# Choosing experts one sequence at a time, and token rows made by transposing back

## The reference, cut to what matters

```python
x = x + ga * attn(layernorm(x) * (1 + ca) + sa)
h = layernorm(x) * (1 + cb) + sb          # the "token rows", 1024 x 256
scores = sigmoid(h @ w_router)            # 1024 tokens x 32 experts
sfc = scores + corr_bias
# 8 groups of 4 experts; a group's score is the sum of its two best; 4 groups are kept,
# and of their experts the 6 best are chosen
topk_idx = top_k(masked(sfc), 6); topk_w = scores[topk_idx]
x = x + gb * (sum over chosen experts of topk_w * expert(h) + shared_experts(h))
```

## Time and profile before

| what | us |
|---|---|
| median of three executions | 492.85 |
| the profiled execution | 493.19 |
| its span, first to last instruction | 491.2 |
| TensorE busy | 415.0 (84%) |
| VectorE busy | 308.1 (63%) |
| ScalarE busy | 193.7 (39%) |
| GpSimd busy | 134.1 (27%) |

### The profile page before, as it was taken

The page is one execution under the profiler, slowest core; times in us unless marked ns, Lnnn a source line. Parts: engine busy times, 40 slices in busy tenths (PEclk is TensorE's granted clock), DMA queues, the critical chain, the costliest instruction groups (busy, mean ns, idle before and its releaser), DMA issues. The chain is left out here.

```text
span 491.2 us, 5968 instructions
## 1 busy us (share of the span) xinstructions
PE 415.0 (84%) x1835; PEld 296.1 (60%) x1836; DVE 308.1 (63%) x718; ACT 193.7 (39%) x336; POOL 134.1 (27%) x145
## 2 busy tenths in 40 slices
PE   2886765788599999999997786489897999799995
PEld 0342054635377777777775535366586777688885
DVE  3489996779344444444443479878678866765432
ACT  2168573424222222222222145281796079322430
POOL 0162000000467777777777302000000000000000
PEclk9999795789699999999999899599999799799998
DMA  8309967693223323333337287602300000000001
GB/s 286 131 20 353 329 158 182 220 372 164 57 77 103 107 96 105 98 107 99 104 118 246 81 304 269 219 1 64 130 0 2 0 0 1 0 1 19 25 0 44
DMA packets 22877, 57.65 MB, mean 117 GB/s; under 512 B 3266, under 2 KB 14020, under 8 KB 21864
## 3 DMA queue, kind: packets, MB, share of 16 engines
q1 hardware_dynamic: 17432, 42.57, 25.6%
q0 software_dynamic: 5424, 14.82, 9.6%
HBM read 46.87 MB, written 10.51 MB: 117 GB/s over the span
## 5 line engine op out<-in xcount | busy, mean ns | idle before, releaser
L659 PE MATMUL bank<-arena,tile_mem 128*128 x224 | 77.4, 469 | 0.0
L1213 POOL DMA_INDIRECT tile_mem<-h_dram,gidx x57 | 55.6, 975 | 55.7 <-DVE gidx L1576 38.2
L1220 POOL DMA_INDIRECT y_dram<-norm,didx x56 | 55.5, 991 | 25.7 <-issue 14.0
L1592 DVE TENSOR_TENSOR tile_mem<-tile_mem,bank 128x176 f32<-128x176 f32 x56 | 18.9, 338 | 69.4 <-ACT tile_mem L1015 69.4
L1171 POOL TENSOR_TENSOR rstd<-ve,mhalf 128x4 f32<-128x4 f32 x8 | 8.1, 1016 | 197.1 <-DVE ve L1333 197.1
L675 PE MATMUL bank<-arena,tile_mem 88*128 x224 | 57.7, 379 | 0.8 <-DVE tile_mem L1587 0.8
L675 PEld LDWEIGHTS bank<-arena,tile_mem 88*128 88x128 f32 x224 | 42.4, 190 | 15.8 <-issue 1.2
L755 PE MATMUL bank<-x_r,f_r 128*128 128x512 f32 x192 | 48.0, 411 | 4.3 <-DVE arena L1767 3.3
L659 PEld LDWEIGHTS bank<-arena,tile_mem 128*128 128x128 f32 x224 | 39.1, 195 | 12.6 <-issue 1.2
L755 PEld LDWEIGHTS bank<-x_r,f_r 128*128 128x128 f32 x192 | 37.4, 197 | 13.8 <-DVE arena L1767 3.7
L1010 ACT ACTIVATE tile_mem<-bank 128x256 f32<-128x256 f32 x57 | 21.9, 385 | 51.9 <-PE bank L652 51.8
(11 more groups left out here) (248 smaller groups left out, 704.1 us busy)
## 6 DMA issues: line engine op xcount, KB each, us to landing
arena<-w_gu SPq DMA_DIRECT2D x3, 2112.0 KB, 12.9
arena<-y_dram SPq DMA_DIRECT2D x8, 768.0 KB, 5.8
arena<-w_dn SPq DMA_DIRECT2D x4, 1408.0 KB
arena<-w_gu SPq DMA_DIRECT2D x2, 2464.0 KB, 17.8
arena<-w_f SPq DMA_DIRECT2D x6, 512.0 KB, 7.3
arena<-w_conv SPq DMA_DIRECT2D x5, 320.0 KB, 5.8
arena<-wmod SPq DMA_DIRECT2D x3, 512.0 KB, 8.5
arena<-wmod SPq DMA_DIRECT2D x2, 768.0 KB, 6.9
```

The lines of the kernel that those rows point to most:

```text
L659: mm = pe.matmul(bank[2 + r % 2][:, 0:2 * M], xgT[r % 2][:, k * P:(k + 1) * P], gu[:, bass.ds(e[k], 2 * M)], start=(k == 0), stop=(k == CT ...
L1213: pool.indirect_dma_start(out=xg[j % 4], out_offset=None, in_=h2_dram, in_offset=bass.IndirectOffsetOnAxis(ap=gidx[:, j:j + 1].bitcast(U32 ...
L1220: pool.indirect_dma_start(out=y_dram, out_offset=bass.IndirectOffsetOnAxis(ap=didx[:, j:j + 1].bitcast(U32), axis=0), in_=yt[j % 4], in_of ...
```

## The change

modB0 and its sb and cb parts go; ga0 and gb0 remain, with four broadcasts. The token rows are no longer computed from norm on VectorE: TensorE transposes hT back (token_rows on TensorE, eight transposes per sequence, into banks 5 and 7 and then 0 and 1), and ScalarE copies the two banks to norm (token_rows on ScalarE) and counts h2_ready. Scores and choice are made per sequence. On TensorE the token_rows of sequence 0 stand between transposes 1 and logits 1, those of sequence 1 between the second and third shared product. On ScalarE the order becomes keep_x(0), modulated 0, scores 0, modulated 1, token_rows 0, scores 1, keep_x(1), first shared silu, token_rows 1.

```diff
@@ -85,6 +85,7 @@
 MOD_BANKS = (2, 3, 4), (0, 1, 4)
 RES_BANKS = (0, 1), (2, 3)
 LN2_BANKS = (5, 7), (0, 1)
+ROW_BANKS = (5, 7), (0, 1)
 RVK_ORDER = ([(c, i) for c in range(CT) for i in range(3)], [(c, i) for i in (0, 2, 1) for c in range(CT)])
...
@@ -170,7 +171,7 @@
         hidT = [tile_mem[0:MH, o + i * 2 * P:o + (i + 1) * 2 * P] for i in range(2)]; o += 2 * C
         yt = [norm[:, TB + r, :] for r in range(4)]
         modrow0 = tile_mem[0:B, 0:6 * C]
-        modB0 = tile_mem[:, 6 * C:6 * C + B * 3 * C].rearrange("p (b n) -> p b n", b=B)
+        ga0 = tile_mem[:, 6 * C:6 * C + B * C].rearrange("p (b n) -> p b n", b=B)
         sh_hid = tile_mem[:, 0:SHT * S].rearrange("p (m n) -> p m n", m=SHT)
         sh_sil = tile_mem[:, SHT * S:(SHT + 1) * S]
...
@@ -403,15 +404,12 @@
             sp_.dma_start(shdn[:, :, :], w_shdn).then_inc(sh_in, 16)
-            sp_.wait_ge(modrow_ready, 3)
-            sp_.dma_start(mod_dram[0][:, SB * C:(SB + 1) * C], modrow0[:, SB * C:(SB + 1) * C]).then_inc(mod_out[0], 16)
-            sp_.wait_ge(modg_ready, 2)
-            sp_.dma_start(modg_dram, modg[0:B, :]).then_inc(mod_out[0], 16)
-            sp_.wait_ge(mod_out[0], 32)
+            sp_.wait_ge(modg_ready, 1)
+            sp_.dma_start(modg_dram, modg).then_inc(mod_out[0], 16)
+            sp_.wait_ge(mod_out[0], 16)
             for b in range(B):
-                for dst, row, at in ((modB0[:, b, 0:C], modg_dram, 0), (modB0[:, b, C:2 * C], mod_dram[0], SB),
-                                     (modB0[:, b, 2 * C:3 * C], modg_dram, 2), (gb0[:, b, :], modg_dram, 1)):
-                    src = row[b:b + 1, at * C:(at + 1) * C].to_broadcast([P, C])
+                for dst, at in ((ga0[:, b, :], 0), (gb0[:, b, :], 1)):
+                    src = modg_dram[b:b + 1, at * C:(at + 1) * C].to_broadcast([P, C])
                     sp_.dma_start(dst, src).then_inc(modB_in[0], 16)
...
@@ -521,6 +519,14 @@
                     for t in range(TB):
                         mm = pe.transpose(bank[banks[c]][:, t * P:(t + 1) * P], norm[:, b * TB + t, c * P:(c + 1) * P], ident)
                     mm.then_inc(normT_done, 1)
+
+            def token_rows(b):
+
+                for t in range(TB):
+                    for c in range(CT):
+                        mm = pe.transpose(bank[ROW_BANKS[b][t // 2]][:, (t % 2) * C + c * P:(t % 2) * C + (c + 1) * P],
+                                          hT[:, c, b * S + t * P:b * S + (t + 1) * P], ident)
+                mm.then_inc(h2T_done, 1)
             def preload_x(b, banks):
...
@@ -580,13 +586,15 @@
             pe.wait_ge(route_in, 32)
             for b in range(B):
                 transposes(B + b, b, (x_done, b) if b else None, LN2_BANKS[b])
-
+                if b:
+                    token_rows(0)
+                    pe.wait_ge(score_ready, b)
                 pe.wait_ge(hT_ready, CT * (B + b + 1))
                 for t in range(b * TB, (b + 1) * TB):
                     for k in range(CT):
                         mm = pe.matmul(bank[6][:, t * E:(t + 1) * E], hT[:, k, t * P:(t + 1) * P], router[:, k, :],
                                        start=(k == 0), stop=(k == CT - 1))
-            mm.then_inc(logit_done, 1)
+                mm.then_inc(logit_done, 1)
             def shared_in(b, parts):
...
@@ -610,10 +618,13 @@
             pe.wait_ge(sh_in, 32)
             pe.wait_ge(x_done, B)
+            shared_in(0, range(2))
+            token_rows(1)
             pe.wait_ge(modcol_ready, 3)
-            shared_in(0, range(3))
-
-            pe.wait_ge(mask_ready, 1)
+            shared_in(0, range(2, 3))
+
+            pe.wait_ge(mask_ready, B)
+            pe.wait_ge(h2_ready, B)
             m16 = mask16[:, :, :].rearrange("p t e -> p (t e)")
             pe.matmul(bank[0][:, 0:NT * E], tri16[:, :], m16, start=True, stop=False, skip_group_check=True)
             for d in range(1, NT):
...
@@ -622,7 +633,7 @@
             for t in range(NT):
                 mm = pe.matmul(bank[1][:, 0:E], ones16[:, :], m16[:, t * E:(t + 1) * E], start=(t == 0), stop=(t == NT - 1))
             mm.then_inc(rank_done, 1)
-            pe.wait_ge(score_ready, 1)
+            pe.wait_ge(score_ready, B)
             shared_in(0, range(3, 2 * SHT))
             pe.wait_ge(ej_ready, 1)
...
@@ -943,8 +954,7 @@
             inverses(1)
             exps(2)
             receptances(1)
-            act.wait_ge(modg_ready, 2)
-            act.wait_ge(mod_out[0], 32)
+            act.wait_ge(modg_ready, 1)
             for n in range(3):
                 act.wait_ge(modps_done, 3 + n + 1)
                 act.activation(modrow1[:, n * 512:(n + 1) * 512], bank[MOD_BANKS[1][n]][0:B, :], ACT.Copy).then_inc(modrow_ready, 1)
...
@@ -969,11 +979,27 @@
             keep_x(0)
             modulated(2, 0, 0, SB, CB, LN2_BANKS[0])
+
+            def token_scores(b):
+
+                act.wait_ge(logit_done, b + 1)
+                act.activation(scores[:, b * TB:(b + 1) * TB, :].rearrange("p t e -> p (t e)"),
+                               bank[6][:, b * TB * E:(b + 1) * TB * E], ACT.Sigmoid).then_inc(score_ready, 1)
+
+            token_scores(0)
             modulated(3, 1, 0, SB, CB, LN2_BANKS[1])
+
+            def token_rows(b):
+
+                act.wait_ge(h2T_done, b + 1)
+                for h in range(2):
+                    t0 = b * TB + 2 * h
+                    ins = act.activation(norm[:, t0:t0 + 2, :].rearrange("p t c -> p (t c)"), bank[ROW_BANKS[b][h]][:, :], ACT.Copy)
+                ins.then_inc(h2_ready, 1)
+
+            token_rows(0)
+            token_scores(1)
             keep_x(1)
-            act.wait_ge(logit_done, 1)
-            act.activation(scores[:, :, :].rearrange("p t e -> p (t e)"), bank[6][:, 0:NT * E], ACT.Sigmoid)\
-               .then_inc(score_ready, 1)
             def shared_silu(b, extra=None):
                 for m in range(SHT):
...
@@ -995,8 +1021,7 @@
                     ins = act.activation(dst, bank[banks[h]][:, :], ACT.Copy)
                 ins.then_inc(shy_ready, 1)
-            act.wait_ge(h2_ready, B)
-            shared_silu(0)
+            shared_silu(0, lambda: token_rows(1))
             for t in range(NT):
                 act.wait_ge(onehot_j_ready, t + 1)
...
@@ -1176,9 +1201,7 @@
             def gate_rows():
                 rows = modrow0.rearrange("p (h c n) -> p h c n", h=2, c=3)[:, :, 2, :]
-                g = modg[0:B, 0:2 * C].rearrange("p (h n) -> p h n", h=2)
-                pool.tensor_scalar(modg[0:B, 2 * C:3 * C], modrow0[:, CB * C:(CB + 1) * C], 1.0, None, ALU.add)\
-                    .then_inc(modg_ready, 1)
+                g = modg.rearrange("p (h n) -> p h n", h=2)
                 step(pool.tensor_scalar(sign0, rows, 0.0, 2.0, ALU.is_ge, ALU.mult))
                 settle()
                 step(pool.tensor_scalar(sign0, sign0, -1.0, None, ALU.add))
...
@@ -1192,12 +1215,12 @@
             def gated_weights():
                 pool.wait_ge(wout_in, 16)
-                pool.wait_ge(modg_ready, 2)
-                pool.wait_ge(modB_in[0], 16 * 4 * B)
+                pool.wait_ge(modg_ready, 1)
+                pool.wait_ge(modB_in[0], 16 * 2 * B)
                 for b in range(B):
                     if b:
                         pool.wait_ge(wg_ready, b)
-                    pool.tensor_tensor(wg[b], wout, modB0[:, b, 0:C].unsqueeze(1).to_broadcast([P, CT, C]), ALU.mult)\
+                    pool.tensor_tensor(wg[b], wout, ga0[:, b, :].unsqueeze(1).to_broadcast([P, CT, C]), ALU.mult)\
                         .then_inc(wg_ready, 1)
             pool.wait_ge(modrow_ready, 3)
...
@@ -1441,64 +1464,61 @@
             sum_stats(1)
             layer_norm(3, x_sum, stats_done=True)
-            dve.wait_ge(modB_in[0], 16 * 4 * B)
-            for b in range(B):
-                dve.wait_ge(normT_done, CT * (B + b + 1))
-                v = norm[:, b * TB:(b + 1) * TB, :]
-                sh, sc = [modB0[:, b, i * C:(i + 1) * C].unsqueeze(1).to_broadcast([P, TB, C]) for i in (1, 2)]
-                step(tt(v, v, sc, ALU.mult))
-                settle()
-                tt(v, v, sh, ALU.add).then_inc(h2_ready, 1)
-
+            dve.wait_ge(modB_in[0], 16 * 2 * B)
+            def choose(b):
+
+                dve.wait_ge(score_ready, b + 1)
+                ts = slice(b * TB, (b + 1) * TB)
+                step(tt(sfc[:, ts, :], scores[:, ts, :], cbias[:, :].unsqueeze(1).to_broadcast([P, TB, E]), ALU.add))
+                settle()
+
+                f4 = sfc[:, ts, :].rearrange("p t (g a b) -> p (t g a) b", g=G, a=2)
...
+                each = range(b * TB, (b + 1) * TB)
+                for t in each:
+                    step(dve.max(gtop[:, t, :], gsx[:, t, :]))
+                settle()
+                for t in each:
+                    step(dve.match_replace(grep[:, t, :], gtop[:, t, :], gsx[:, t, :], -BIG))
...
+                for t in each:
+                    step(dve.max(stop8[:, t, :], sfx[:, t, :]))
```

(61 more changed lines are left out.)

29 lines of the change are left out of this document (24 added, 5 removed).

## The result

| | runs | us, median (lowest to highest) | profiled execution: time, span, mean clock |
|---|---|---|---|
| before | 4 | 492.01 (490.09 to 494.07) | 493.19, 491.2, 0.927 |
| after | 4 | 484.52 (484.06 to 484.99) | 484.72, 482.8, 0.944 |

The ratio is 0.9896, with a 95% interval of 0.9853 to 0.9938: 7.5 us less, against the 1.4 us forecast. Four later comparisons of the same two kernels, with 10 or 12 runs of after in each, gave 0.9971, 0.998, 0.997 and 0.9965, which is 1.0 to 1.8 us. So two things have to be explained: what the change does, and what the other 6 us were.

A forecast was written before the change was run, and what follows sets the result against it. The expert loop keeps TensorE busy and its start hangs on VectorE's gather indices, set by the end of the ranks plus one product. Attention −0.8 and router −0.6 sum to −1.4 us, giving 491.4 us as a median, range 487.5 to 495.0.

The forecast's parts named there:

- Attention: Attention stretch: GpSimd's multiplications start earlier, about 39.8 us, and disturb VectorE less; 0.8 us gained.
- undisturbed: Attention stretch: the best-case bound, VectorE not slowed beside GpSimd at all; 1.9 us gained.
- the 0.4 that I estimated by it: Attention stretch: by the shared-port rule scans with two SBUF inputs wait too; 0.4 us gained instead of 0.8.
- Choice: Router, VectorE: choice in halves of 5.25 us; half 1 ends at 102.0 instead of 105.04, ending no wait.
- To the ranks: Router: TensorE's own queue, its first product waiting for keep_x(1), puts the ranks at 106.2 instead of 105.10.
- Behind the ranks: Router: fourth product at full clock, 1.7 us not 3.6; VectorE's small work ends at 109.0 against 109.61.
- Router part in all: Router, to the end of VectorE's small work after the ranks: 0.6 us gained (1.4 gained to 0.1 lost).
- Store and late loads: SyncE: token rows 1's store lands by 110.7, needed 112.2; loads end about 123, needed near 130; costed at nothing.
- The rival with the store: Slower rival, before the one-hots: VectorE waits for token rows 1's store, 5.6 us late; 497.0 us, chance 0.10.
- The clock is kept: Faster rival, router: transposes in TensorE's pause keep 2.4 GHz past 92.2; 3.8 us gained in all, 489.0, chance 0.28.
- the one that made the total: Whole kernel: −1.4 us against the profiled 493.19 gives 491.8; that execution lies 0.34 above the median, so 491.4.
- The sum of the change: Whole kernel: −0.8 us in attention and −0.6 us in the router part give −1.4 us.

The follow-up runs named there:

- e3: The kernel before with the attention half of the change alone, its token-row values not the reference's; ratio to before 0.9952 (0.9913 to 0.9992).
- e4: The changed kernel with the attention half undone; ratio to before 0.996 (0.9923 to 0.9997).
- e7: The changed kernel with the choice made whole again, everything else left; ratio to before 0.9981 (0.9943 to 1.0019).
- e1: The kernel before, unchanged, profiled a second time; ratio to before 0.9976 (0.9942 to 1.0009).
- e17: The kernel before with 20 unread products in TensorE's pause before the last attention projection; 486.20 us against 488.56, ratio 0.9941 (0.9915 to 0.9968).
- e2: The changed kernel, unedited, profiled and timed again; ratio to before 0.9971 (0.9933 to 1.0009).
- e5: The changed kernel, unedited, timed in more rounds; ratio to before 0.998 (0.9944 to 1.0016).
- e12: The changed kernel, unedited, once more; 486.84 us (484.42 to 490.16 in 12 runs), ratio to before 0.997 (0.9938 to 1.0003).
- e16: The changed kernel, unedited, as the mark for runs with filled pauses; ratio to before 0.9965 (0.9932 to 0.9998).
- e11: The changed kernel with keep_x(1) put back ahead of the second sigmoid; 484.30 us, ratio to before 0.990 (0.9861 to 0.9938).
- e13: The kernel before with 36 unread products in TensorE's pause before the last attention projection; ratio to before 1.0138 (1.0067 to 1.021).
- e14: The changed kernel with 36 unread products in TensorE's pause before the last attention projection; ratio to before 1.0054 (1.0004 to 1.0104).
- e18: The changed kernel with keep_x(1) ahead of the second sigmoid and 20 unread products before the last attention projection; ratio to before 0.9919 (0.9887 to 0.9952).
- e9: The kernel before with eight unread transposes added ahead of the second logits; ratio to before 0.9996 (0.9957 to 1.0035).
- e8: The changed kernel without the token rows' transposes and copies, its gathered values not the reference's; ratio to before 1.0004 (0.9966 to 1.0042).

## Why the prediction was right and wrong

The forecast was 491.4 us, in 487.5 to 495.0; 484.52 came out, below the range.

- **Attention: 0.8 gained was forecast, 0.63 came** (0.56 to 0.60 by e3, 0.06 to 0.48 by e4). The mechanism was right, with GpSimd's start at 37.27 where I had 39.8: 1.86 us of that is the earlier start of the program, 0.7 is left. It met other instructions than I had supposed, a product and a scan. The bound "undisturbed" fell: the scan took 1.70 us beside GpSimd. The rule of the Trainium skill (SBUF — State Buffer, "SBUF: two separate sides"), by which scans with two SBUF inputs wait too, agrees with that row; the 0.4 that I estimated by it and my 0.8 lie on either side of the 0.63.
- **Choice: 5.25 us per half, mask 3 us earlier, ending no wait.** Half 1 took 92.48 to 97.94, 5.46 us, and the mask stood ready 3.4 us before the ranks. e7 shows that the split is worth nothing here.
- **To the ranks: the mis-sized term.** Counted from norm 1, I had them at 17.6 us (106.2 less 88.62); they came at 16.53 (101.37 less 84.84), 16.48 before. Three parts make up the 1.1 us. The token rows' transposes didn't fit the pause (logits started 5.23 us behind norm 1, 4.15 before), but the clock rose during them, so the logits took 2.07 instead of 3.62 and ended half a us sooner than forecast: the first product began at 8.73, not 9.2. The first two products took 5.2 us and not 5.6, transposes and third product 2.6 and not 2.8.
- **Behind the ranks: 2.8 us to the fourth product's result, as forecast** (101.37 to 104.18). Router part in all: 0.6 forecast, 1.65 came. How much of this belongs to the change depends on where the clock stands: the code of before took 37.60, 37.58 (e1), 36.34 (e3) and 35.92 (e17) there, while seven profiles of the changed order (after, e2, e4, e5, e7, e12, e16) gave 35.94 or 35.95. So it is 1.65 us where the clock falls as in before, and nothing against e17.
- **Store and late loads: costed at nothing, and nothing they cost.** No wait of VectorE or TensorE ended on them. The rival with the store fell.
- **The clock is kept** (0.28): half true. It fell at 87.1, inside the transposes, was back at 90.5 for the logits, and fell again at 93.9, behind the new 1.44 us wait for keep_x(1). I had named that wait as the argument against this rival; in e11, which removes it, the clock still falls at 88.0, but once up at 91.4 it stays, and the router part is 4.2 us under before's 37.60, where the rival had 3.0.
- **The step that failed is the one that made the total**: the sum was set against one execution of 493.19 us, the stretches outside the change were held fixed, and the scatter of one kernel was taken as 2 us from three runs. The kernel before ran from 485.48 to 494.25 us (34 runs), the changed one from 484.42 to 490.16 (e12). Four stretches of the same code gave 5.7 of the 8.4 us between the two profiles.
- **What moved in these four stretches.** For the one between the norms the cause is shown: the projection takes 5.09 us (e11) to 6.63 (before) when the clock rises inside it and 3.62 to 3.72 when it doesn't have to (e13, e14, e17, e18). In the loop 0.72 of the 1.23 us lie between its first two products on VectorE: 3.11 us in before, where the clock came up only at 136.5, 2 us into the loop, against 2.39 in after, where it was up at 128.0, ahead of it; e9 and e17, code of before with the rise at 134.6 and 130.6, have 2.71 and 2.38. At the start 1.82 of the 1.86 us lie between VectorE's first two copies of the modulation (12.35 to 18.25 in before, 12.31 to 16.39 in after), where TensorE's eight transposes at 13.60 took 1.97 us against 1.09 in after and in e1; that is their length at half clock (1.97 in e11 at 87.99), yet the profiles give a granted clock of 1.00 there, so the cause is argued only. Behind the loop it stays open. e1, which is the kernel before, has 24.16 at the start and 208.11 behind the loop, below after's values, so these two differences don't belong to the change.
- **The sum of the change agrees with the later comparisons, and partly by luck.** −1.4 us is a ratio of 0.997; the four gave 0.9965 to 0.998, but their intervals reach from 0.9932 to 1.0016, which is 3.3 us gained to 0.8 lost. Its router term was 0.6 where 0 to 1.65 came. That the first comparison's 0.9896 was timing and a small sample fits all five. It is not separately shown, and chance alone is a weak account of it: all four of its runs of after are below 485, where only 2 of e12's 12 are.

## What to carry to other kernels

Before a small change is priced, compare two executions of the same kernel stretch by stretch: what moves there by itself is the least width that a range can have, and three runs don't show it. Look at each new wait on TensorE for what it does to the clock of the work behind it: here moving one 1.08 us copy of ScalarE ahead of a sigmoid was worth 2.6 us in the router part, more than all the rest of the change, as long as the clock was up for the work behind it; in e18, with the same order, it was down and the gain was gone. And filling a pause pays where it keeps the clock for a projection (e17), but each such filling has to be measured to the end, since the clock can be lost further on (e18).

## What the runs showed of the hardware

- The clock came back sooner where transposes filled the pause before the second logits. In after it went from 0.50 to 1.00 at 90.5 us, behind 16 transposes and 0.4 us of logits, with no other product since 86.2; in e9 at 93.6, also behind 16. In e8, with eight transposes less and a pause in their place, it stayed at 0.50 until 99.2. In all, twelve profiles with these transposes have a fall beside them and the rise by the end of the second logits; in six without them (before, e1, e3, e8, e13, e17) it came only during the shared products behind. It doesn't always work: e18 has the same 16 transposes with TensorE busy throughout, and 0.50 until 97.6. Whether other work in that pause would do the same was not tried.
- At some times every kernel, before's too, took about 522 us. Two of the chips gave 488.56 and 489.63 us for the kernel before at one time and 522.83 and 522.40 at another, so it isn't the chip alone. The difference lies in the expert loop, some 180 us instead of 146, where TensorE's weight loads stood for no reason that the profile names: 22.9 of the 35 us are idle time before one group of them. The row of line 686's loads, in e12 and then in e16, the same kernel (busy us, mean ns | idle before, what ended it):

```profile
L686 PEld LDWEIGHTS bank<-arena,tile_mem 88*128 88x128 f32 x224 | 42.4, 190 | 15.8 <-issue 1.0
```

```profile
L686 PEld LDWEIGHTS bank<-arena,tile_mem 88*128 88x128 f32 x224 | 42.6, 195 | 38.7 <-issue 27.2
```

The cause stays open.
